# Normalising attention probabilities on GpSimd before the mix, instead of scaling the mix on VectorE

## Chip, cores and metric

One core of a Trainium2 chip runs the whole program. The metric is the device time of one execution in microseconds (us); the kernel before was run three times.

## The reference, cut to what matters

The program is a chain of attention and feed-forward layers over x of shape (2, 1024, 256), float32. The change lies in two of them, both called "local" in the kernel. Each has this attention, with 8 heads of 64 columns (D) and windows of 128 rows; a window of queries sees its own and the previous window of keys:

```python
q = l2norm(q) * qs
k = l2norm(k) * ksc
q, k = rotary_xpos(q, k)
...
sim = jnp.einsum('bhwid,bhwjd->bhwij', bq, bk)      # bq is scaled by 8
sim = jnp.where(mask, -jnp.finfo(sim.dtype).max, sim)
attn = jax.nn.softmax(sim, axis=-1)
out = jnp.einsum('bhwij,bhwjd->bhwid', attn, bv)
...
x = x + o @ wo
```

The softmax's division by the sum can be applied to the probabilities (256 columns a head and row) or, as it is linear, to the mix `out` (64 columns a head and row).

## The kernel before, in words

local_attention (L3100 on) handles 16 tiles of 128 rows (T = 16, 8 for each of the two batch entries). All engines run their own queue, written out by hand: every_step(T, (lag, body), ...) calls in each of 16 steps s the bodies in the order given, each for the tile s - lag. After the 16 steps the remaining pieces of the last tiles (LAST = 15) are listed one by one. Semaphores connect the queues; `x.at(t, name)` is the value that means "x of tile t is done".

What one tile goes through:

- TensorE: turn (L3393) transposes the input into the bank c; ScalarE's copy_h (L3322) brings it to SBUF. project_q, project_k and project_v (L3399) multiply with the weights into the banks q, k and v. project_q and project_k wait until ScalarE's copy_qk of the tile before has left these banks.
- VectorE: rope_q and rope_k (L3219, L3221, L3224) apply the rotation; norms (L3235, L3238) sums ScalarE's squares (L3353); GpSimd's power (L3169) makes the inverse norms of queries and keys; VectorE applies the keys' (L3245).
- One step later turn_qk (L3422) transposes both into the banks q and k, ScalarE's copy_qk (L3333, L3335) copies them to SBUF, and score (L3440) fills the four score banks.
- Two steps later VectorE's maxima (L3255, L3260) masks, takes row maxima and writes biases; ScalarE's exp (L3344) makes eight blocks of 128x256 probabilities, one a head, with their row sums. Semaphore steps "0" to "3" of exped mark two heads each, so that "1" means heads 0 to 3 and "3" all. turn_p (L3456) transposes the probabilities into the score banks, ScalarE's copy_p (L3359) copies them out (for the last tiles partly VectorE, L3283), mix (L3472) multiplies with the values into the bank c, and ScalarE's copy_o (L3327) copies the mix to o.
- The division: VectorE's invert (L3266) takes reciprocals of the eight sums, GpSimd's spread_inv (L3174) copies them to 64 columns a head, three steps behind TensorE's turn_inv (L3481) transposes this into the bank v in four transposes, and VectorE's scale_o (L3272) multiplies o with that bank into o_t. output (L3487) multiplies o_t with the output weights, add (L3277) adds the input, and SP shifts the result by DMAs. In layer 0 VectorE's norm_next (L3192) normalises the input of the tile after next; layer 1 has no such instruction.

TensorE's order in a step is turn, turn_qk, turn_inv, project_q, output, project_k, turn_p, project_v, mix, score. VectorE's order is maxima, scale_o, rope_q, add, norm_next, norms, invert, rope_k, and in the last two steps statistics (L3069, L3072, L3074) for the feed-forward that follows. ScalarE's order is copy_h, copy_qk, exp, square, copy_p, copy_v, copy_o. GpSimd's is spread_inv and power. A feed-forward stage follows each of the two attention stages and starts when all engines are through.

## Time and profile before

| | us |
|---|---|
| median of three runs | 2340.4 |
| lowest, highest | 2330.86, 2352.32 |
| the profiled execution, its own time | 2345.13 |
| its span in the trace | 2343.4 |

A profile shows one execution. Times in it are us from the start of the span. PE is TensorE's matmuls, PEld its weight loads, DVE VectorE, ACT ScalarE, POOL GpSimd, SP SyncE. The first local attention stage lies at about 613 to 864 us and the second at about 990 to 1245 us.

### The profile page before, as it was taken

The numbers are of one execution on the slowest core, as the hardware profiler recorded it, in microseconds if no ns is written. First come the engines' busy times: TensorE is split into PE (matmuls) and PEld (weight loads), VectorE is DVE, ScalarE is ACT, GpSimd is POOL, SyncE is SP. The second block draws the span as 40 slices with busy tenths as digits, with TensorE's granted clock in tenths as the row PEclk, the third lists the DMA queues.
The fourth block names the chain that finished last, engine by engine and source line by source line (L and its number), as shares of the span: only waits on it lengthen the run. The fifth ranks groups of instructions, "written<-read, shape, count | busy, mean of one in ns | idle before, by whom it ended". The sixth has DMA issues, their size and how long they took to land. (4 is left out here: it accounts for less than half of the span.)

```text
span 2343.4 us, 39319 instructions
## 1 busy us (share of the span) xinstructions
PE 2099.3 (90%) x12889; PEld 1560.0 (67%) x12889; DVE 1094.8 (47%) x4126; ACT 936.1 (40%) x2964; POOL 615.2 (26%) x553
## 2 busy tenths in 40 slices
PE   7888889987699989889998969969999699599998
PEld 4565548765366655556664558858887477499997
DVE  4555424438577753267773347822222355412111
ACT  3344313324377752157773225412221366333332
POOL 0455525652222210022221002222223112312222
PEclk9777779998799999999999979969999799799999
DMA  8500029988590020000000054111221801276662
GB/s 289 216 7 28 14 80 313 342 243 293 182 368 15 11 66 0 15 28 11 11 10 6 0 203 144 40 41 28 36 35 17 287 21 42 78 244 181 179 179 52
DMA packets 161423, 255.35 MB, mean 109 GB/s; under 512 B 37548, under 2 KB 123984, under 8 KB 160311
## 3 DMA queue, kind: packets, MB, share of 16 engines
q1 hardware_dynamic: 131798, 224.62, 27.8%
q0 software_dynamic: 29424, 28.21, 6.8%
q8 instruction: 107, 1.75, 0.3%
q14 instruction: 94, 0.76, 0.1%
HBM read 165.95 MB, written 101.04 MB: 114 GB/s over the span
## 5 line engine op out<-in xcount | busy, mean ns | idle before, releaser
L2736 ACT ACTIVATE m3e_ht<-m3e_h_bank,m3w_b 128x128 f32<-128x128 f32 x312 | 89.2, 368 | 189.0 <-PE m3e_h_bank L2708 187.2
L3344 ACT ACTIVATE la_probs<-la_probs,la_nb,la_invnorm 128x256 f32<-128x256 f32 x256 | 150.2, 594 | 0.0
L926 POOL DMA_INDIRECT m_xbuf<-m0w_rows,m0w_slots x128 | 127.1, 993 | 65.6 <-issue 36.3
L2719 PE MATMUL m3e_y_bank<-m3w_w,m3e_ht 128*128 x624 | 141.0, 379 | 0.0
L2890 ACT ACTIVATE m2e_ht<-m2e_h_bank,m2w_b 128x270 f32<-128x270 f32 x128 | 62.2, 487 | 179.0 <-PE m2e_h_bank L2855 179.0
L2428 POOL DMA_INDIRECT m_sum<-m0e_y,m0e_dest x64 | 98.8, 1544 | 106.6 <-DVE m0e_y L2600 75.3
L2719 PEld LDWEIGHTS m3e_y_bank<-m3w_w,m3e_ht 128*128 128x128 f32 x624 | 115.7, 190 | 14.1
L2683 POOL DMA_INDIRECT out<-m3e_y,m3e_dest x39 | 60.4, 1549 | 238.7 <-DVE m3e_y L2771 230.7
L2830 POOL DMA_INDIRECT m_sum<-m2e_y,m2e_dest x48 | 70.2, 1463 | 199.6 <-DVE m2e_y L2938 194.2
L2855 PE MATMUL m2e_h_bank<-m2e_xt,m2w_w 128*128 128x270 f32 x512 | 121.4, 395 | 0.0
L2748 DVE COPY m3e_xt<-m3e_turned_bank 128x256 f32<-128x256 f32 x39 | 16.5, 424 | 220.0 <-PE m3e_turned_bank L2696 220.0
L2865 PE MATMUL m2e_y_bank<-m2e_ht,m2w_w 128*128 128x270 f32 x512 | 119.3, 391 | 0.0
L2855 PEld LDWEIGHTS m2e_h_bank<-m2e_xt,m2w_w 128*128 128x128 f32 x512 | 96.9, 192 | 19.1
L2865 PEld LDWEIGHTS m2e_y_bank<-m2e_ht,m2w_w 128*128 128x128 f32 x512 | 96.0, 190 | 18.3
L3174 POOL COPY la_spread<-la_inv 128x512 f32<-128x512 f32 x32 | 19.5, 611 | 325.2 <-DVE la_inv L3266 325.2
L3169 POOL TENSOR_TENSOR la_invnorm<-la_clamped,all_minushalf 128x16 f32<-128x16 f32 x32 | 92.9, 2902 | 35.2 <-DVE la_clamped L3238 35.2
L3255 DVE CUSTOM_DVE_ANT_0 la_probs<-la_score_bank,lo_shut 128x256 f32<-128x256 f32 x256 | 97.9, 420 | 6.4 <-PE la_score_bank L3440 5.3
L2453 PE MATMUL m0e_gu_bank<-m0e_xt,m0w_wgu 128*128 128x128 f32 x768 | 92.5, 278 | 0.0
L2708 PE MATMUL m3e_h_bank<-m3e_xt,m3w_w 128*128 128x128 f32 x768 | 91.2, 278 | 0.2 <-DVE m3e_xt L2748 0.2
L2453 PEld LDWEIGHTS m0e_gu_bank<-m0e_xt,m0w_wgu 128*128 128x128 f32 x768 | 89.6, 194 | 0.6 <-issue 0.6
L2708 PEld LDWEIGHTS m3e_h_bank<-m3e_xt,m3w_w 128*128 128x128 f32 x768 | 89.0, 194 | 0.6 <-DVE m3e_xt L2748 0.6
L3631 PE MATMUL lf_g_bank<-lf_zt,lo_w 128*128 128x512 f32 x160 | 79.3, 620 | 7.5 <-DVEq L3549 7.5
(504 smaller groups left out, 4850.0 us busy)
## 6 DMA issues: line engine op xcount, KB each, us to landing
m3w_w<-in_m_w SPq DMA_DIRECT2D x32, 1024.0 KB, 9.4
m0w_wgu<-in_m_gu SPq DMA_DIRECT2D x32, 768.0 KB
m_xbuf<-all_zeros SPq DMA_DIRECT2D x38, 528.0 KB, 6.0
m2w_w<-in_m_w SPq DMA_DIRECT2D x16, 1024.0 KB, 12.6
m3e_w<-in_m_w SPq DMA_DIRECT2D x15, 1024.0 KB, 6.7
m0e_wd<-in_m_down SPq DMA_DIRECT2D x32, 384.0 KB
m_xbuf<-all_zeros SPq DMA_DIRECT2D x16, 576.0 KB, 7.7
m0w_xb<-m_xbuf SPq DMA_DIRECT2D x32, 288.0 KB
```

What stands on the lines that cost most here:

```text
L926: nc.gpsimd.indirect_dma_start(k.slot_buffers[m.name][0][:, :], bass.IndirectOffsetOnAxis(ahead.slots[:, t, i:i + 1], 0), ahead.rows[t % R ...
L2428: nc.gpsimd.indirect_dma_start(sums[j][:, :], bass.IndirectOffsetOnAxis(dest[q % NY][:, i:i + 1], 0), y[q % NY][:, i, :], None, bounds_che ...
L2453: last = nc.tensor.matmul(gu_ps[u][:, i * 512 + j * P:i * 512 + (j + 1) * P], wgu[q % NG][:, i * DC + c, j * P:(j + 1) * P], xt[u][:, c, i ...
L2708: last = nc.tensor.matmul(h_ps[t % 2][half][:, i * R:(i + 1) * R], w1[t % NW][:, c, f0:f0 + P], xt[t % 2][:, c, :], start=c == 0, stop=c = ...
L2719: last = nc.tensor.matmul(y_ps[t % 2][0:R, 0:D], h_t[t % 2][:, c, :], ahead.w2[:, bass.ts(e, 1), c, :].rearrange("p o f -> p (o f)"), star ...
L2736: last = nc.scalar.activation(h_t[t % 2][:, 4 * half + i, :], h_ps[t % 2][half][:, i * R:(i + 1) * R], m.act, bias=ahead.b1[:, bass.ds(e * ...
L2855: last = nc.tensor.matmul(h_ps[n % 3][:, 0:N], ahead.w1[:, h // 2, c, f * P:(f + 1) * P], xt[h % 2][:, c, :], start=c == 0, stop=c == DC - 1)
L2865: last = nc.tensor.matmul(y_ps[c][:, 0:N], ahead.w2[:, h // 2, f, c * P:(c + 1) * P], h_t[h % 2][:, f, :], start=f == 0, stop=f == HC - 1)
L3169: nc.gpsimd.tensor_tensor(inv_norm[t % 2][:, :], clamped[t % 2][:, :], k.minus_half[:, :], ALU.pow).then_inc(powered.sem, 1)
L3255: last = nc.vector.tensor_tensor_reduce(probs[u][:, hh, :], score_ps[j][:, i * 2 * P:(i + 1) * 2 * P], lo.shut[:, int(t % TB == 0), :], 1. ...
L3344: last = nc.scalar.activation(probs[u][:, hh, :], probs[u][:, hh, :], ACT.Exp, bias=nb[u][:, hh:hh + 1], scale=inv_norm[u][:, hh:hh + 1], ...
L3631: last = nc.tensor.matmul(ps[:, :], w1[:, dc, i, :], z_t[g % 2][:, dc, :], start=dc == 0, stop=dc == DC - 1)
```

## The change

The reciprocals multiply the probabilities themselves, before they are transposed. GpSimd does it in place, head by head, in eight tensor_scalar instructions of 128x256 a tile: four after the sums of heads 0 to 3 (scale_low), four after those of heads 4 to 7 (scale_high). VectorE takes the reciprocals in two halves, invert_low directly behind maxima and invert_high behind norm_next. The spread reciprocals, their transposes (turn_inv) and the scaled mix (scale_o, with the buffers spread and o) go; ScalarE copies the mix straight into o_t, and output waits for that copy. On TensorE turn_p, mix and score are split into halves, and the order of a step becomes turn, turn_qk, project_q, output, project_k, turn_low, project_v, turn_high, mix_low, score_low, mix_high, score_high. At the end of the loop the pieces keep their order, without turn_inv and scale_o, with both reciprocals of tile 14 behind the maxima of tile 15.

```diff
@@ gpsimd
-                def spread_inv(t):
-                    pool.wait_ge(inverted.sem, inverted.at(t, "inverted"))
-                    pool.wait_ge(inv_turned.sem, inv_turned.at(t - 1, "invturned"))
-                    nc.gpsimd.tensor_copy(spread[:, :, :], inv[t % 2][:, :].unsqueeze(2).broadcast_to([P, LH, LD])).then_inc(spreading.sem, 1)
+                def scale_probs(t, j):
+                    pool.wait_ge(inverted.sem, inverted.at(t, f"{j}"))
+                    for hh in range(2 * (j - 1), 2 * (j - 1) + 4):
+                        last = nc.gpsimd.tensor_scalar(probs[t % 2][:, hh, :], probs[t % 2][:, hh, :], inv[t % 2][:, hh:hh + 1], None, ALU.mult)
+                    last.then_inc(scaled.sem, 1)
...
-                every_step(T, (2, spread_inv), (0, power), (0, power_forward))
+                every_step(T, (2, scale_low), (2, scale_high), (0, power), (0, power_forward))
@@ vector
-                def invert(t):
-                    dve.wait_ge(exped.sem, exped.at(t, "3"))
-                    dve.wait_ge(spreading.sem, spreading.at(t - 2, "spreading"))
-                    nc.vector.reciprocal(inv[t % 2][:, :], total[t % 2][:, :]).then_inc(inverted.sem, 1)
-
-                def scale_o(t):
-                    dve.wait_ge(o_copied.sem, o_copied.at(t, "ocopied"))
-                    dve.wait_ge(inv_turned.sem, inv_turned.at(t, "invturned"))
-                    dve.wait_ge(made.sem, made.at(t - 1, "made"))
-                    nc.vector.tensor_tensor(o_t[:, :, :], o[:, :, :], v_ps[:, :].rearrange("p (c n) -> p c n", c=4),
-                                            ALU.mult).then_inc(o_scaled.sem, 1)
+                def invert(t, j):
+                    h0 = 2 * (j - 1)
+                    dve.wait_ge(exped.sem, exped.at(t, f"{j}"))
+                    dve.wait_ge(scaled.sem, scaled.at(t - 2, f"{j}"))
+                    nc.vector.reciprocal(inv[t % 2][:, h0:h0 + 4], total[t % 2][:, h0:h0 + 4]).then_inc(inverted.sem, 1)
...
-                every_step(T, (2, maxima), (3, scale_o), (0, rope_q), (3, add), (0, norm_next), (0, norms), (2, invert), (0, rope_k), (0, forward_stats), steps=T)
+                every_step(T, (2, maxima), (2, invert_low), (0, rope_q), (3, add), (0, norm_next), (2, invert_high), (0, norms), (0, rope_k),
+                           (0, forward_stats), steps=T)
                 maxima(LAST - 1)
-                scale_o(LAST - 2)
                 maxima(LAST)
+                invert_low(LAST - 1)
+                invert_high(LAST - 1)
                 forward.norm(dve, 0)
                 forward.norm(dve, 1)
                 add(LAST - 2)
-                invert(LAST - 1)
                 copy_p(LAST - 1, range(4))
                 for t in range(2, 4):
                     forward.stats(dve, t)
-                scale_o(LAST - 1)
-                invert(LAST)
+                invert_low(LAST)
+                invert_high(LAST)
                 copy_p(LAST, (2, 3))
                 add(LAST - 1)
                 for t in range(2, 4):
                     forward.norm(dve, t)
-                scale_o(LAST)
                 add(LAST)
@@ scalar
                 def copy_o(t):
                     act.wait_ge(mixed.sem, mixed.at(t, "mixed"))
-                    act.wait_ge(o_scaled.sem, o_scaled.at(t - 1, "oscaled"))
-                    nc.scalar.copy(o[:, :, :], c_ps[:, :].rearrange("p (c n) -> p c n", c=4)).then_inc(o_copied.sem, 1)
+                    act.wait_ge(made.sem, made.at(t - 1, "made"))
+                    nc.scalar.copy(o_t[:, :, :], c_ps[:, :].rearrange("p (c n) -> p c n", c=4)).then_inc(o_copied.sem, 1)
@@ tensor, turn_p
                         pe.wait_ge(exped.sem, exped.at(t, f"{j0 + 1}"))
+                        pe.wait_ge(scaled.sem, scaled.at(t, f"{j0 + 1}"))
@@ tensor
-                every_step(T, (0, turn), (1, turn_qk), (3, turn_inv), (0, project_q), (3, output), (0, project_k), (2, turn_p), (0, project_v), (2, mix), (1, score), steps=T)
+                every_step(T, (0, turn), (1, turn_qk), (0, project_q), (3, output), (0, project_k), (2, turn_low), (0, project_v), (2, turn_high),
+                           (2, mix_low), (1, score_low), (2, mix_high), (1, score_high), steps=T)
                 turn_qk(LAST)
-                turn_inv(LAST - 2)
                 score(LAST)
                 output(LAST - 2)
                 turn_p(LAST - 1)
...
                 mix(LAST - 1)
                 turn_p(LAST)
-                turn_inv(LAST - 1)
                 output(LAST - 1)
                 mix(LAST)
...
-                turn_inv(LAST)
                 output(LAST)
```

## Rows read from the trace of the kernel before

**Rows 1.** Page, first part: engine, busy us, share of the span, instructions.
```profile
PE 2099.3 (90%) x12889; PEld 1560.0 (67%) x12889; DVE 1094.8 (47%) x4126; ACT 936.1 (40%) x2964; POOL 615.2 (26%) x553
```

**Rows 2.** Windows: busy us (instructions) of PE, PEld, DVE, ACT, POOL; PE clock; DMA.
```profile
...
744.54:758.77 14.23, 14.17 (x134) 9.72 (x130) 11.17 (x37) 10.42 (x28) 3.47 (x2) 1.00 0.04 10
```

**Rows 3.** Timeline, a usual step of layer 0: start us, us, engine, line, out<-in.
```profile
737.01 0.59 ACT L3333 COPY la_qt<-la_q_bank 128x512 f32<-128x512 f32 x1
...
737.25 0.60 PE L3481 MATMUL la_v_bank<-all_ident,la_spread 128*128 128x128 f32 x4
...
737.75 1.96 PE L3399 MATMUL la_q_bank<-lo_wqkv,la_ht 128*128 128x512 f32 x4
...
739.02 0.69 DVE L3272 TENSOR_TENSOR la_ot<-la_o,la_v_bank 128x512 f32<-128x512 f32 x1
...
739.74 0.69 DVE L3219 TENSOR_TENSOR la_cosed<-la_q_bank,lo_cosq 128x512 f32<-128x512 f32 x1
...
740.23 0.19 ACT L3344 ACTIVATION_READ_ACCUMULATOR la_probs<-la_probs,la_nb,la_invnorm 128x1 f32 x1
...
742.13 0.41 DVE L3192 TENSOR_SCALAR lo_y<-all_x,all_mv,all_rstd 128x256 f32<-128x256 f32 x1
...
742.57 0.19 ACT L3344 ACTIVATION_READ_ACCUMULATOR la_probs<-la_probs,la_nb,la_invnorm 128x1 f32 x1
...
743.40 1.21 PE L3456 MATMUL la_score_bank<-all_ident,la_probs 64*128 64x64 f32 x32
...
745.78 2.90 POOL L3169 TENSOR_TENSOR la_invnorm<-la_clamped,all_minushalf 128x16 f32<-128x16 f32 x1
...
746.43 0.69 DVE L3224 TENSOR_TENSOR la_qk<-la_cosed,la_sined 128x512 f32<-128x512 f32 x1
```

**Rows 4.** Timeline, output in steps 3 and 15 of layer 0; idle before in brackets.
```profile
654.33 1.99 PE L3487 MATMUL la_v_bank<-lo_wo,la_ot 128*128 128x256 f32 x8 [0.65 <-DVE la_ot L3272]
...
825.93 1.99 PE L3487 MATMUL la_v_bank<-lo_wo,la_ot 128*128 128x256 f32 x8 [0.83 <-DVE la_ot L3272]
```

**Rows 5.** Groups by line of GpSimd, whole span: busy us, mean ns, idle before.
```profile
L3169 POOL TENSOR_TENSOR la_invnorm<-la_clamped,all_minushalf 128x16 f32<-128x16 f32 x32 | 92.9, 2902 | 35.2 <-DVE la_clamped L3238 35.2
...
L3174 POOL COPY la_spread<-la_inv 128x512 f32<-128x512 f32 x32 | 19.5, 611 | 325.2 <-DVE la_inv L3266 325.2
...
L3164 POOL MEMSET all_zeros<- 128x1152 f32 x1 | 1.2, 1205 | 0.0
```

**Rows 6.** Timeline, the end of layer 0's attention, tiles 14 and 15.
```profile
844.79 0.16 DVE L3260 SCALAR_TENSOR_TENSOR la_nb<-la_mx,la_invnorm 128x2 f32<-128x2 f32 x1
...
844.82 1.21 PE L3456 MATMUL la_score_bank<-all_ident,la_probs 64*128 64x64 f32 x32 [0.81 <-DVE la_mx L3255]
...
845.86 0.20 DVE L3266 RECIPROCAL la_inv<-la_total 128x8 f32<-128x8 f32 x1
...
845.98 2.43 DVE L3283 COPY la_probst<-la_score_bank 128x512 f32<-128x512 f32 x4
...
849.49 1.22 PE L3456 MATMUL la_score_bank<-all_ident,la_probs 64*128 64x64 f32 x32
...
849.95 0.15 DVE L3074 TENSOR_SCALAR lf_ve<-lf_mv 128x1 f32<-128x1 f32 x1
...
852.13 1.99 PE L3487 MATMUL la_v_bank<-lo_wo,la_ot 128*128 128x256 f32 x8 [0.84 <-DVE la_ot L3272]
...
854.05 1.97 PE L3472 MATMUL la_c_bank<-la_probst,la_v 128*64 128x128 f32 x32
...
857.13 0.58 ACT L3327 COPY la_o<-la_c_bank 128x512 f32<-128x512 f32 x1
...
858.49 1.99 PE L3487 MATMUL la_v_bank<-lo_wo,la_ot 128*128 128x256 f32 x8 [1.44 <-DVE la_ot L3272]
```

**Rows 7.** Timeline, scores of the last tile, layer 0 and layer 1.
```profile
840.03 2.06 PE L3440 MATMUL la_score_bank<-la_kt,la_qt 64*128 64x128 f32 x32 [2.00 <-DVE la_mx L3255]
...
1220.93 3.42 PE L3440 MATMUL la_score_bank<-la_kt,la_qt 64*128 64x128 f32 x32 [1.99 <-DVE la_mx L3255]
```

More of the change, by code:

```diff
@@ L3158, in _ @@
             def _(pool):
[L3159 removed]
+                for st in (powered, scaled, forward.powered):
                     pool.sem_inc(st.sem, 2 * st.n)
@@ L3432, in score @@
                     pe.wait_ge(qk_copied.sem, qk_copied.at(t, "k"))
-                    for j0 in (0, 2):
+                    for j0 in ((0, 2) if half is None else (half,)):
                         for i in range(2):
@@ L3443, in score, with score_low, score_high, turn_p @@
                                         last.then_inc(scored.sem, 1)
-                def turn_p(t):
+                def score_low(t):
+                    score(t, 0)
+                def score_high(t):
+                    score(t, 2)
+                def turn_p(t, banks=(0, 2)):
                     if t == LAST - 1:
@@ L3459, in turn_p, with turn_low, turn_high, mix @@
                                         last.then_inc(p_turned.sem, 1)
-                def mix(t):
-                    u = t % 2
+                def turn_low(t):
+                    turn_p(t, (0,))
+                def turn_high(t):
+                    turn_p(t, (2,))
+                def mix(t, chunks=range(4)):
                     pe.wait_ge(v_copied.sem, v_copied.at(t, "vcopied"))
@@ L3465, in mix @@
                     pe.wait_ge(o_copied.sem, o_copied.at(t - 1, "ocopied"))
-                    for c in range(4):
+                    for c in chunks:
                         if c % 2 == 0:
@@ L3473, in mix, with mix_low, mix_high, output @@
                                                         probs_t[:, hh, w, :], start=w == 0, stop=w == 1, skip_group_check=True)
-                    last.then_inc(mixed.sem, 1)
-                def turn_inv(t):
-                    pe.wait_ge(spreading.sem, spreading.at(t, "spreading"))
+                    if 3 in chunks:
+                        last.then_inc(mixed.sem, 1)
+                def mix_low(t):
+                    mix(t, (0, 1))
+                def mix_high(t):
+                    mix(t, (2, 3))
+                def output(t):
+                    pe.wait_ge(o_copied.sem, o_copied.at(t, "ocopied"))
                     pe.wait_ge(added.sem, added.at(t - 1, "added"))
@@ L3480, in turn_inv @@
                     for c in range(4):
-                        last = nc.tensor.transpose(v_ps[:, c * P:(c + 1) * P], spread[:, 2 * c:2 * c + 2, :].rearrange("p h e -> p (h e)"), k.ident[:, :])
-                    last.then_inc(inv_turned.sem, 1)
-                def output(t):
-                    pe.wait_ge(o_scaled.sem, o_scaled.at(t, "oscaled"))
-                    for c in range(4):
                         last = nc.tensor.matmul(v_ps[:, 0:D], o_t[:, c, :], wo[:, c, :], start=c == 0, stop=c == 3)
                     last.then_inc(made.sem, 1)
-                every_step(T, (0, turn), (1, turn_qk), (3, turn_inv), (0, project_q), (3, output), (0, project_k), (2, turn_p), (0, project_v), (2, mix), (1, score), steps=T)
+                every_step(T, (0, turn), (1, turn_qk), (0, project_q), (3, output), (0, project_k), (2, turn_low), (0, project_v), (2, turn_high),
+                           (2, mix_low), (1, score_low), (2, mix_high), (1, score_high), steps=T)
                 turn_qk(LAST)
-                turn_inv(LAST - 2)
                 score(LAST)
```

28 lines of the change are left out of this document (17 added, 11 removed).

## The prediction

> **What bounds the kernel now.** I read the page first: TensorE is busy for 90% of the span, so what counts is whether its queue ever stands still [rows 1]. The change touches only the two attention stages of the local layers, each a loop of 16 steps. The windows view over one step, cut at the start of the value projection, gives 14.23 us with TensorE busy for 14.17 of them, VectorE for 11.17, ScalarE for 10.42 and GpSimd for 3.47, at full clock [rows 2]. So in these steps TensorE has no holes, and nothing counts that doesn't shorten or interrupt its queue. The timeline of that step then says what each piece of the queue waits for [rows 3]; timelines of the first and last steps show the few holes that there are [rows 4].
>
> **Part 1, the four turns of the spread reciprocals go (turn_inv).** They take TensorE from 737.25 to the projection of the queries at 737.75 [rows 3], about 0.5 us, in steps 3 to 15 of each layer: 13 x 2 x 0.5 = 13 us if it were all won. It isn't. project_q writes the bank of the queries, so it waits for ScalarE's copy of that bank, which runs 737.01 to 737.60; its matmul starts 0.15 us after that. The turns fill a wait that stays when they go. From the copy's end with 0.06 us for the semaphore and about 0.03 for the first weight load, the projection could start about 0.06 us earlier, no more. Term: 13 x 0.06 = -0.8 us a layer. What is late next is the chain turn_qk, copy of q, project_q; the new hole of some 0.5 us has only this small value.
>
> **Part 2, VectorE's scaling of the mix goes (scale_o, 0.69 us), and output no longer waits for it.** In a usual step it runs 739.02 to 739.71 and output follows when project_q's matmuls end anyway (737.75 + 1.96 = 739.71), so nothing is won there. In step 3 TensorE stood 0.65 us for it and in step 15 0.83 us, there because VectorE had other work in front [rows 4]. These waits go: -1.5 us a layer. The pieces mix_low, score_low, mix_high, score_high hold the same matmuls as mix and score; TensorE had no wait for the copies there in a usual step, so the new order wins nothing.
>
> **Part 3, GpSimd multiplies eight 128x256 blocks a step.** The trace has no GpSimd tensor_scalar. Near rows: its copy of 128x512 takes 611 ns, 1.19 ns a column, its memset of 1152 columns 1205 ns, 1.05 a column. The other way lies its pow, 2902 ns for 16 columns [rows 5]. From below: half the copy, 0.31 us. From above: the pow's 181 ns a column would make 46 us of 256 columns (8 blocks in 16 steps of two layers: some 12 ms more). That is a power, which takes many operations an element, while a product takes one; so the value lies by far nearer to the copy, which streams one tensor as the product does. From that far end the range takes only blocks up to about 0.8 us, more than twice the copy's rate. I take 0.45 us each, half above the copy's rate, for the multiplication and the scalar of each partition. Four then take 1.8 us.
> The Trainium skill, "GPSIMD Engine Reference", section 3.1, gives about 1.8 cycles an element for a tight loop: as an estimate 384 ns for 256 elements and a little for dispatch. By it the sum below would stay the same within a microsecond; no row here shows it.
>
> Does this reach TensorE's queue? Low half: the fourth exponential's sum is read by 740.42 (740.23 + 0.19). VectorE, idle after its maxima, now waits there, takes 0.20 for the reciprocal (0.20, [rows 6]), and GpSimd starts at about 740.74 and ends at 742.54. TensorE comes to the low turns at 743.40 less 0.06 = 743.34 [rows 3]. Slack 0.8 us; it holds up to 0.64 us a block. High half: VectorE's wait delays rope_q from 739.74 to 740.68. From rope_q's start to the end of norm, with add between, are 2.80 us (739.74 to 742.13 + 0.41) [rows 3]; so the high reciprocal ends at 743.68 (the eighth exponential's sum is done at 742.57 + 0.19), GpSimd starts at 743.74 and ends at 745.54. TensorE reaches the high turns after the low turns (half of 1.21) and the value projection (1.96, as project_q): 745.9. Slack 0.3 us; it holds up to 0.52 us a block, in the second layer, where norm is absent, to 0.6. Queued behind the two new VectorE waits are rope_q, add, norm_next and the norms. rope_q's sines are still done before ScalarE's squares (742.0 against 742.66), add ends about when norm starts, 742.13 + 0.94 = 743.1, and the value projection needs it at 743.9. GpSimd's own queue behind the scaling is the pow (745.78 before, behind the spread copy); it now starts at 745.5 and isn't late. So a usual step stays at about 14.17 us.
>
> **Part 4, the end of each layer, where nothing hides GpSimd.** Times of layer 0 [rows 6]. VectorE's last bias ends at 844.95; only then come both reciprocals of tile 14 (they stand behind the maxima of tile 15). GpSimd works 845.2 to 848.8 (8 x 0.45), the high turns end at 849.5 instead of 846.03 (844.82 + 1.21). VectorE's last two of the four copies (0.61 each) end at 850.75 instead of 848.41. Its statistics keep 1.69 us (848.41 to 850.10), the reciprocals of tile 15 end at 852.65, GpSimd 852.7 to 856.3, and the turns of tile 15 end at 857.0 instead of 850.71. output(14), now behind them, starts at 856.95 instead of 852.13: +4.8 us. The mix of tile 15 moves with it from 854.05 to 858.9, ScalarE's copy from 857.13 to 861.95, ending 862.54, and the last output starts at 862.6 instead of 858.49, as scale_o is no more between: +4.1 us a layer. With 0.31 us a block it would be 16 x 0.14 = 2.2 us less, +1.9.
> TensorE now stands about 2 us before each of the two turns. After such a hole the scores of the last tile took 3.42 us in layer 1, and 2.06 in layer 0 [rows 7]: a lower clock costs up to 1.4 us a time. I take one such loss, +1.4; between 0 and 4 x 1.4.
>
> **Sum.** A layer: -0.8 - 1.5 + 4.1 = +1.8, two layers +3.6, clock +1.4: +5 us. The profiled execution took 2345.1 us (span 2343.4), so 2350.1; the median of the three runs is 4.7 us below it, so 2345 on that scale. A measurement of this kernel can tell about 1% (23 us; the runs shown lie 21 us apart), so I forecast no change.
>
> **Rivals.**
> A, GpSimd is slow (slower). If a block takes 0.8 us, low scaling ends at 743.94 and the low turns wait 0.66 us; the high scaling then runs to 747.14 while TensorE is there at 746.6: another 0.6. Some 1.3 us in each of the 14 steps from step 2 of both layers is 36 us, the ends take 16 x 0.35 x 2 = 11.2 more: 2345 + 47 = 2392 us. It decides from about 0.66 us a block (there 9 us in the steps and 7 at the ends beyond the forecast's +5). For it: pow shows that GpSimd's arithmetic can be far from its copy. Against it: copy and memset both run near 1.1 ns a column. 0.20.
> B, GpSimd and VectorE hinder each other. rope_q's last addition (0.69 us, two tensors of SBUF) would fall in the low scaling, which would end at 743.23, still before 743.34; the addition itself may wait for one block, so the high scaling ends 0.45 later at 745.99, TensorE waits 0.2 us, in 14 steps of two layers 5.6 us: 2351 us; with blocks of 0.6 us it would be some 0.9 us a step, 2370. Against it: the pow (745.78 to 748.68) overlaps such an addition in every step, at 746.43 for instance, which takes the same 0.69 us as other 512-column operations [rows 3]. The Trainium skill, "SBUF — State Buffer", says that a VectorE instruction with two SBUF inputs and a GpSimd instruction that reads SBUF exclude one another for their whole length; the trace has only the pow beside it and shows no such price. 0.15.
> C, the freed 0.5 us is won in full: 13 x 2 x 0.44 = 11 us more, 2334 us. This needs ScalarE's copy to end before TensorE is through with the turns, and rows 3 speak against it. 0.05.
> D, the loop isn't as tight as drawn and 0.7 us a step goes somewhere: faster by over 1%. Nothing shows it. 0.04.
>
> **How the numbers follow.** Forecast 0.56, A 0.20, B 0.15, C 0.05, D 0.04. Forecast, C and nearly all of B lie within 1%; A and a small part of B are slower by more, as are blocks between 0.5 and 0.66 us with a bad clock: 0.23. Faster 0.04, same 0.73. The range goes from 2326 (C and the scatter of the runs) to 2390 (most of A).
>
> **What would show it.** The step's pitch stays between 14.1 and 14.3 us with 13.6 us of TensorE busy in it; TensorE waits for ScalarE's query copy before project_q, about 0.5 us; waits for GpSimd at the low and high turns are zero in the steps and 1.5 to 3 us four times at the layers' ends; the scaling blocks measure 0.4 to 0.5 us. A pitch near 13.7 would make part 1 wrong, waits of turn_low or turn_high in every step part 3, an unmoved end of the layers part 4.

## The result, and the profile after

| | us |
|---|---|
| before, median (lowest, highest) of 3 runs | 2340.4 (2330.86, 2352.32) |
| after, median (lowest, highest) of 3 runs | 2464.86 (2462.63, 2465.87) |
| ratio after / before, 95% interval | 1.0517 [1.0478, 1.0555] |
| the profiled execution after, its own time and span | 2465.87, 2464.1 |

The change makes the kernel 5.2% slower; the profiled execution takes 120.7 us more than that of before (2345.13). I had forecast 2345 us, no change, and the time lies beyond my range (2326 to 2390). It went the way of rival A, and further than A's price.

The page of after, its first part and then the two groups of the change (GpSimd's scaling, TensorE's turns of the probabilities):

```profile
span 2464.1 us, 39398 instructions
...
PE 2113.9 (86%) x12761; PEld 1565.5 (64%) x12761; DVE 1075.7 (44%) x4126; ACT 933.4 (38%) x2964; POOL 844.6 (34%) x777
...
L3173 POOL TENSOR_SCALAR la_probs<-la_probs,la_inv 128x256 f32<-128x256 f32 x256 | 247.3, 985 | 209.1 <-DVE la_inv L3273 209.1
...
L3469 PE MATMUL la_score_bank<-all_ident,la_probs 64*128 64x64 f32 x1024 | 48.8, 238 | 108.6 <-POOL la_probs L3173 108.6
```

TensorE's busy time rose by only 14.6 us against [rows 1], while the span rose by 120.7: most of the loss is TensorE standing. The second group puts 108.6 us of it down to waits for GpSimd's scaling. The first group has the reason: a block takes 985 ns in the mean, where I had reckoned 450.

The windows view of one step, cut as [rows 2] at the start of the value projection:

```profile
754.24:771.76 17.52, 14.21 (x130) 9.57 (x127) 10.45 (x37) 10.36 (x27) 10.77 (x10) 1.00 0.03 9
```

TensorE still does 14.21 us of work at full clock, but the step takes 17.52 instead of 14.23. GpSimd went from 3.47 us to 10.77. The waits of this stretch, in total, times, longest:

```profile
DVE la_qk L3251 <- POOL la_invnorm L3168: 4.7, 1, 4.7
...
PE la_score_bank L3469 <- POOL la_probs L3173: 3.0, 2, 1.5
...
PE la_q_bank L3405 <- ACT la_qt L3339: 0.3, 1, 0.3
```

14.21 + 3.0 + 0.3 = 17.5: the step is accounted for. Its timeline, a usual step of layer 0 as in [rows 3]:

```profile
746.00 0.59 ACT L3339 COPY la_qt<-la_q_bank 128x512 f32<-128x512 f32 x1
...
746.74 1.96 PE L3405 MATMUL la_q_bank<-lo_wqkv,la_ht 128*128 128x512 f32 x4 [0.33 <-ACT la_qt L3339]
...
749.44 0.18 DVE L3273 RECIPROCAL la_inv<-la_total 128x4 f32<-128x4 f32 x1 [2.15 <-ACT la_probs L3350]
...
749.72 7.88 POOL L3173 TENSOR_SCALAR la_probs<-la_probs,la_inv 128x256 f32<-128x256 f32 x8 [6.75 <-DVE la_inv L3273]
...
750.91 0.73 DVE L3230 TENSOR_TENSOR la_qk<-la_cosed,la_sined 128x512 f32<-128x512 f32 x1
...
752.22 0.16 DVE L3273 RECIPROCAL la_inv<-la_total 128x4 f32<-128x4 f32 x1
...
753.59 0.71 PE L3469 MATMUL la_score_bank<-all_ident,la_probs 64*128 64x64 f32 x16 [1.46 <-POOL la_probs L3173]
...
755.22 0.69 DVE L3230 TENSOR_TENSOR la_qk<-la_cosed,la_sined 128x512 f32<-128x512 f32 x1
...
757.57 2.92 POOL L3168 TENSOR_TENSOR la_invnorm<-la_clamped,all_minushalf 128x16 f32<-128x16 f32 x1
757.74 0.71 PE L3469 MATMUL la_score_bank<-all_ident,la_probs 64*128 64x64 f32 x16 [1.52 <-POOL la_probs L3173]
```

The high reciprocal is ready at 752.38, when the low scaling still runs; so the eight blocks follow one another without a gap, 7.88 us, and TensorE stands 1.46 us at the low turns and 1.52 at the high ones. VectorE's scaling of the keys, which waits 4.7 us for the pow behind these blocks, ends at 761.28, before TensorE turns the keys in the next step, and costs nothing.

Six of the eight blocks take 0.92 us. The third takes 1.02, beside VectorE's norm_next (a tensor_scalar, 751.90 to 752.30); without norm_next, in layer 1, a step is 0.1 us shorter. The seventh stands out; the same timeline of GpSimd alone, at 755.23:

```profile
755.23 1.47 POOL L3173 TENSOR_SCALAR la_probs<-la_probs,la_inv 128x256 f32<-128x256 f32 x1
```

It begins 0.01 us behind rope_k's last addition (755.22, two operands of SBUF) and takes 0.55 us more than the others.

The end of layer 0, the part that answers to [rows 6] (with the scores of the last tile, [rows 7], first):

```profile
888.11 3.65 PE L3446 MATMUL la_score_bank<-la_kt,la_qt 64*128 64x128 f32 x32 [1.95 <-DVE la_mx L3261]
...
893.87 0.28 DVE L3273 RECIPROCAL la_inv<-la_total 128x4 f32<-128x4 f32 x2
...
894.15 7.35 POOL L3173 TENSOR_SCALAR la_probs<-la_probs,la_inv 128x256 f32<-128x256 f32 x8 [8.94 <-DVE la_inv L3273]
...
898.05 0.95 PE L3469 MATMUL la_score_bank<-all_ident,la_probs 64*128 64x64 f32 x16 [4.37 <-POOL la_probs L3173]
...
901.65 1.12 PE L3469 MATMUL la_score_bank<-all_ident,la_probs 64*128 64x64 f32 x16 [2.65 <-POOL la_probs L3173]
...
905.97 7.21 POOL L3173 TENSOR_SCALAR la_probs<-la_probs,la_inv 128x256 f32<-128x256 f32 x8 [4.46 <-DVE la_inv L3273]
...
909.73 1.11 PE L3469 MATMUL la_score_bank<-all_ident,la_probs 64*128 64x64 f32 x16 [3.35 <-POOL la_probs L3173]
...
913.32 1.12 PE L3469 MATMUL la_score_bank<-all_ident,la_probs 64*128 64x64 f32 x16 [2.48 <-POOL la_probs L3173]
...
914.37 3.78 PE L3506 MATMUL la_v_bank<-lo_wo,la_ot 128*128 128x256 f32 x8
```

The four waits at the turns are those that I had drawn, only longer, and the clock falls beside them. Windows over two of these rows (before the last two numbers stands the granted clock):

```profile
888.00:891.70 3.70, 3.59 (x33) 3.50 (x33) 1.50 (x11) 3.70 (x14) 0.00 (x0) 0.54 0.00 0
...
914.40:918.20 3.80, 3.80 (x12) 2.61 (x12) 1.30 (x3) 0.00 (x0) 0.00 (x0) 0.50 0.00 0
```

The scores of the last tile and the output run near or at 1.2 GHz, half the full clock: 3.65 us where before had 2.06, 3.78 where before had 1.99. For the scores the record doesn't show that this comes from the change: TensorE stood as long ahead of them before (2.00 us), and in layer 1 they took 3.42 us before and 2.91 after.

From TensorE's first turn to the last addition, layer 0 took 247.9 us before (613.09 to 860.94) and takes 308.1 now (616.48 to 924.57): +60.2, half of the whole loss. Fourteen steps at 3.29 us each (17.52 - 14.23) are 46 of it; 14 are left for the end and the first steps. Layer 1, where a step takes 17.42 us, gives +57.4 in the same way.

### The profile page after: what moved, and what is told of

Read it like the earlier page. It is cut to its first block and busy times, and to the rows that moved or that the text cites. A ratio compares the mean times of both kernels' runs of the same rounds, so it can differ in the third digit from the quotient of the medians.

```text
span 2464.1 us, 39398 instructions
## 1 busy us (share of the span) xinstructions
PE 2113.9 (86%) x12761; PEld 1565.5 (64%) x12761; DVE 1075.7 (44%) x4126; ACT 933.4 (38%) x2964; POOL 844.6 (34%) x777
## 5 line engine op out<-in xcount | busy, mean ns | idle before, releaser
L3173 POOL TENSOR_SCALAR la_probs<-la_probs,la_inv 128x256 f32<-128x256 f32 x256 | 247.3, 985 | 209.1 <-DVE la_inv L3273 209.1
L3469 PE MATMUL la_score_bank<-all_ident,la_probs 64*128 64x64 f32 x1024 | 48.8, 238 | 108.6 <-POOL la_probs L3173 108.6
L3469 PEld LDWEIGHTS la_score_bank<-all_ident,la_probs 64*128 64x128 f32 x1024 | 41.4, 148 | 156.5 <-issue 156.5
L2719 PEld LDWEIGHTS m3e_y_bank<-m3w_w,m3e_ht 128*128 128x128 f32 x624 | 115.7, 190 | 14.1
L3365 ACT COPY la_probst<-la_score_bank 128x512 f32<-128x512 f32 x116 | 62.3, 589 | 133.3 <-PE la_score_bank L3469 133.3
```

The costliest lines, as they stand in the source:

```text
L2719: last = nc.tensor.matmul(y_ps[t % 2][0:R, 0:D], h_t[t % 2][:, c, :], ahead.w2[:, bass.ts(e, 1), c, :].rearrange("p o f -> p (o f)"), star ...
L3173: last = nc.gpsimd.tensor_scalar(probs[t % 2][:, hh, :], probs[t % 2][:, hh, :], inv[t % 2][:, hh:hh + 1], None, ALU.mult)
L3469: last = nc.tensor.transpose(score_ps[j0 + half][:, c0:c0 + QH], probs[t % 2][q0:q0 + QH, 2 * j0 + i, w * P:(w + 1) * P], k.ident[q0:q0 + ...
```

## The experiments

The theory after this reading: GpSimd's block is too long (0.92 us alone), and rope_k's addition holds one of eight for another 0.55. Rivals: the new order of the pieces costs by itself; or the block's length is a price of the instruction as such, and not of its columns. "Pitch" is the time from one step to the next in the middle of layer 0. The runs were compared with the kernel before on the same chip.

### e1_one_column: GpSimd scales one column of each head

```diff
-                        last = nc.gpsimd.tensor_scalar(probs[t % 2][:, hh, :], probs[t % 2][:, hh, :], inv[t % 2][:, hh:hh + 1], None, ALU.mult)
+                        last = nc.gpsimd.tensor_scalar(probs[t % 2][:, hh, 0:1], probs[t % 2][:, hh, 0:1], inv[t % 2][:, hh:hh + 1], None, ALU.mult)
```

The other 255 columns stay without their reciprocal. Every instruction, wait and place in the order stays.

> GpSimd scales one column of each head instead of 256, so most of the normalisation is left out; queues, waits and order are those of the changed kernel. Theory L (the loss is GpSimd's block of 0.98 us, which stands before both turns of every step and 16 times in a row at each layer's end): the step's pitch falls from 17.52 us to 14.1-14.2 us, both waits for GpSimd in a step are gone, the 0.3-0.5 us wait of project_q for ScalarE's copy of the queries stays, and the time is about 2332-2340 us, within 0.5% of the kernel before. Rival O (the loss lies in the new order, in VectorE's early wait for the exponentials or in the halves): the pitch stays above 15 us and the time above 2370 us. Rival F (the removed turns are a gain of 0.5 us a step that the scaling hides): pitch 13.7 us, about 2325 us.

Measured: 2344.41 us, ratio 0.9993 [0.9965, 1.002], pitch 14.40. A block:

```profile
L3173 POOL TENSOR_SCALAR la_probs<-la_probs,la_inv x256: 272/282/420, 639.1 to 1235.2; 128x1 f32<-128x1 f32 x128
```

The waits for GpSimd in the steps are gone, and with them the whole loss. The new order by itself makes no difference to the time that these runs can tell. The pitch is 0.17 us above that of before, where I had expected 14.1 to 14.2 us (see e5 and e9).

### e2_half_width: 128 of 256 columns

Edit: as e1, with `0:P`. Half of each head's columns stays unscaled.

> GpSimd scales 128 of the 256 columns of each head (half of the normalisation is left out). If a block costs by its columns it takes 0.45-0.55 us, the length on which the forecast was built. Theory L: pitch 14.2 to 14.4 us, waits for GpSimd in a step at most 0.2 us, time 2340-2355 us, so the schedule of the prediction was right and only the block's length wrong. Rival O (order): pitch above 15 us. If the block has a large fixed cost (0.7 us or more for half the columns) the pitch is 15 us or more, with the waits at the turns to show it.

Measured: 2387.06 us, 1.018 [1.0139, 1.0221], pitch 15.22. My expectation missed (2340 to 2355 us, pitch 14.2 to 14.4): a block takes a little longer than I had set, and something else comes with it.

```profile
L3173 POOL TENSOR_SCALAR la_probs<-la_probs,la_inv x256: 592/601/1111, 637.1 to 1268.3; 128x128 f32<-128x128 f32 x128
```

With 272, 592 and 912 ns at the least for 1, 128 and 256 columns, both halves give 2.5 ns a column (320 / 127 and 320 / 128) on 0.27 us that don't depend on them. So it is a straight line, more than twice as steep as the copy of [rows 5] (1.19 ns a column).

The longest block, 1111 ns, shows what else there is. A step of this run, the block from GpSimd's timeline:

```profile
791.67 1.11 POOL L3173 TENSOR_SCALAR la_probs<-la_probs,la_inv 128x128 f32<-128x128 f32 x1
...
791.69 0.70 DVE L3230 TENSOR_TENSOR la_qk<-la_cosed,la_sined 128x512 f32<-128x512 f32 x1
...
793.65 0.71 PE L3469 MATMUL la_score_bank<-all_ident,la_probs 64*128 64x64 f32 x16 [0.74 <-POOL la_probs L3173]
```

Here the held block is one of the low half, beside rope_q's addition, and TensorE stands 0.74 us at the low turns and not at all at the high ones. The block is 0.51 us too long, and the one behind it, beside norm_next, takes 0.75 us, 0.15 too long. So 0.66 of the 0.74 us is VectorE's doing: with undisturbed blocks of 0.60 us TensorE would have stood under 0.1 us. That is rival B in its own place, and near the 0.9 us a step that it set for blocks of 0.6.

### e4_end_only: full width only for the last two tiles

```diff
+                        cols = 2 * P if t >= LAST - 1 else 1
-                        last = nc.gpsimd.tensor_scalar(probs[t % 2][:, hh, :], ...
+                        last = nc.gpsimd.tensor_scalar(probs[t % 2][:, hh, 0:cols], ...
```

Tiles 0 to 13 stay unscaled but for a column.

> GpSimd scales all 256 columns only for the last two tiles (14 and 15) of each layer and one column for the others (the normalisation of the others is left out). Against the run with one column everywhere this gives the price of the layers' ends alone. Theory L: 16 blocks of 0.92 us stand on the path of each end, 14-15 us a layer less what hides there, so 24-30 us over the one-column run, about 2362 us. Rival (the ends hide the blocks behind the last maxima and exponentials): under 8 us over the one-column run.

Measured: 2366.19 us, 1.0089 [1.0055, 1.0122], pitch 14.40 as e1. The two ends cost 2366.19 - 2344.41 = 22 us, a little less than the 24 to 30 that I had expected; the steps cost the rest.

### e3_short_add: both rope additions cut to 64 columns

```diff
-                    nc.vector.tensor_tensor(qk[:, i, :].rearrange("p (h e) -> p h e", h=LH), cosed[:, i, :, :], sined[:, i, :, :],
-                                            ALU.add).then_inc(roped.sem, 1)
+                    nc.vector.tensor_tensor(qk[:, i, 0:LD], cosed[:, i, 0, :], sined[:, i, 0, :], ALU.add).then_inc(roped.sem, 1)
```

Seven of eight heads' queries and keys stay at zero (one memset ahead of the loop); the scaling is that of the change.

> The two additions of the rotation on VectorE (two SBUF inputs, 512 columns, 0.69 us) are cut to 64 columns; the rest of the queries and keys is left out (zero). GpSimd's blocks stay 256 columns. Theory C (the block that starts right behind such an addition is held for it: one block of the eight takes 1.47 us instead of 0.92): no block above 1.05 us, the eight take 7.3-7.5 us instead of 7.88, pitch about 17.0 us, time 14-18 us below the changed kernel, about 2448 us. Rival (the long block has another cause, or the length is the engine's own scatter): long blocks stay, pitch 17.4-17.5 us, time unchanged.

Measured: 2440.72 us, 1.0417 [1.0374, 1.0459], pitch 17.06. That is 0.46 us a step less than the change, some 13 us in 28 steps. The median is 24 us lower, more than the 14 to 18 that I had expected, but not all of it is the edit's: from the first turn of layer 0 to the last addition of layer 1 the profiled run took 735.6 us (605.73 to 1341.32), against 745.8 after the change (616.48 to 1362.27), 10 us less, and another 11 were gone ahead of that first turn. The block's span of lengths shows where the 0.46 us come from; the first row is the change, the second this run:

```profile
L3173 POOL TENSOR_SCALAR la_probs<-la_probs,la_inv x256: 912/922/1476, 644.6 to 1350.6; 128x256 f32<-128x256 f32 x128
```

```profile
L3173 POOL TENSOR_SCALAR la_probs<-la_probs,la_inv x256: 913/922/1053, 634.2 to 1328.7; 128x256 f32<-128x256 f32 x128
```

The longest goes from 1476 to 1053 ns (blocks of this length lie beside norm_next, one of 1.03 us at 704.64), and the median stays. TensorE's two waits tell which addition it is:

```profile
706.71 0.72 PE L3469 MATMUL la_score_bank<-all_ident,la_probs 64*128 64x64 f32 x16 [1.46 <-POOL la_probs L3173]
...
710.39 0.72 PE L3469 MATMUL la_score_bank<-all_ident,la_probs 64*128 64x64 f32 x16 [1.05 <-POOL la_probs L3173]
```

At the low turns, beside rope_q's addition, nothing changed (1.46); at the high turns, beside rope_k's, 1.52 became 1.05. So with blocks of 0.92 us it is rope_k's addition that costs. The shorter addition also makes VectorE's own queue shorter; that doesn't reach the eight blocks, which run without a gap either way. In both runs in which a block is held (e2, the change) the addition and the block start within 0.02 us of one another; rope_q's addition in the change starts 0.28 us into a block and no block is held.

### e6_filler: four transposes back where turn_inv was

One column as in e1, and TensorE turns the identity four times into the bank of the values between turn_qk and project_q.

```diff
+                def filler(t):
+                    pe.wait_ge(added.sem, added.at(t - 1, "added"))
+                    pe.wait_ge(v_copied.sem, v_copied.at(min(t + 2, T - 1), "vcopied"))
+                    for c in range(4):
+                        nc.tensor.transpose(v_ps[:, c * P:(c + 1) * P], k.ident[:, :], k.ident[:, :])
-                every_step(T, (0, turn), (1, turn_qk), (0, project_q), (3, output), ...
+                every_step(T, (0, turn), (1, turn_qk), (3, filler), (0, project_q), (3, output), ...
```

> One column scaled (normalisation left out), and four transposes of the identity into the value bank stand between turn_qk and project_q, where the turns of the reciprocals had been. Hidden wait: these four, 0.5 us by themselves, cost at most 0.15 us a step (pitch 14.4-14.55 us), project_q's wait for the copy is gone. Rival F (the turns' time counts in full): pitch 14.9 us, 13 us more.

Measured: 2346.22 us, 1.0112 [0.9962, 1.0261] (the interval is wide and says little), pitch 14.40, as e1 to the hundredth. The turns and what stands behind them:

```profile
781.22 0.60 PE L3505 MATMUL la_v_bank<-all_ident 128*128 128x128 f32 x4
781.72 1.96 PE L3405 MATMUL la_q_bank<-lo_wqkv,la_ht 128*128 128x512 f32 x4
```

The wait for the query copy is gone and the pitch has not moved: the four turns fill exactly the hole that they leave.

### e5_output_first: that hole filled with output

One column as in e1, and output stands ahead of project_q.

```diff
-                every_step(T, (0, turn), (1, turn_qk), (0, project_q), (3, output), (0, project_k), ...
+                every_step(T, (0, turn), (1, turn_qk), (3, output), (0, project_q), (0, project_k), ...
```

> One column scaled (normalisation left out), and TensorE's output stands before project_q. In the one-column run the pitch is 14.40 us, and project_q starts 0.94 us behind the last turn of the keys, with a wait of 0.33 us for ScalarE's copy of the queries. If that wait is a true hole which the removed turns of the reciprocals had filled, output fills it: pitch 14.0-14.1 us, no such wait, about 8 us less than the one-column run. Rival (the wait is a mark of the profile and the turns were a true gain): pitch unchanged at 14.4 us.

Measured: 2335.43 us, 1.0003 [0.9952, 1.0055], pitch 14.11 by this window:

```profile
778.20:792.31 14.11, 13.87 (x127) 9.48 (x127) 10.34 (x38) 10.19 (x28) 5.03 (x9) 1.00 0.04 10
```

That is 0.29 us a step less than e1, so output did have slack to be moved; the value projection then waits 0.24 us for the addition instead. Eight microseconds in all are below what the scatter of these runs lets one tell (2320 to 2346).

### e9_whole: mix and score whole again

One column as in e1, with mix and score undivided behind turn_high.

> One column scaled (normalisation left out), and TensorE's mix and score are whole again (turn_p stays in halves around the value projection). In the one-column run the four halves take 4.23 us from the first mix to the next turn, the whole ones of the kernel before 3.88, with the same matmuls. If each change between groups of matmuls costs TensorE about 0.1 us, the pitch falls from 14.40 to 14.05-14.25 us (the second half of mix may now wait up to 0.2 us for the last copy of the probabilities). Rival (the extra 0.17 us over the kernel before has another source, VectorE's early wait or the late copies): pitch 14.4 us or more.

Measured: 2343.26 us, 1.0001 [0.9972, 1.0031], pitch 14.41: the expectation missed. Making mix and score whole wins nothing. TensorE in a step of e9:

```profile
781.42 0.71 PE L3469 MATMUL la_score_bank<-all_ident,la_probs 64*128 64x64 f32 x16
782.07 2.33 PE L3490 MATMUL la_c_bank<-la_probst,la_v 128*64 128x128 f32 x32
```

The whole mix takes 2.33 us here, against 1.97 in before ([rows 6]), as its last weight loads wait 0.4 us for ScalarE's last copy of the turned probabilities; mix and score together take 4.24 us from start to start (782.07 to 786.31). That copy is later because turn_high stands directly ahead of mix instead of a value projection. The halves hide this wait and pay for it otherwise: in e1 the four half pieces take 4.23 us from start to start (787.60 to 791.83), the two whole ones in before 3.88. In e9 the wait is the whole excess of 0.36 us over before; what the 0.35 us of e1 consist of, these runs don't separate.

### e7_vector and e8_split: the scaling on VectorE, and shared

Both compute everything. e7 puts the eight blocks on VectorE, directly behind each reciprocal; e8 gives two heads of each half to VectorE and two to GpSimd.

```diff
+                    for hh in range(h0, h0 + 4):
+                        last = nc.vector.tensor_scalar(probs[t % 2][:, hh, :], probs[t % 2][:, hh, :], inv[t % 2][:, hh:hh + 1], None, ALU.mult)
+                    last.then_inc(scaled.sem, 1)
```

> VectorE scales all eight blocks itself, behind each half's reciprocals; GpSimd keeps only the power. Full computation. VectorE's 128x256 tensor_scalar took 0.41 us with two scalars (0.34 apart); at 0.33 us a block a half costs 1.3 us in place of GpSimd's 3.7-4.1, but it stands in VectorE's own queue before rope_q and the norms: the two waits for the scaling at the turns are gone, add and the rotation come 1.3-2.6 us later, and the pitch is 14.5-15.0 us, 2355-2380 us. If a block takes 0.2 us or less, pitch 14.4 us, within 0.5% of the kernel before. Rival (the block on GpSimd isn't what costs, but the wait of TensorE for any scaling at all): pitch above 16 us.

> Of each half VectorE scales two heads and GpSimd two at the same time. Full computation. By length alone GpSimd's part is 1.84 us a half, 8 us in all at the ends: pitch 14.6-15.0 us, about 2365-2380 us. If the two engines exclude one another while VectorE's one-input instruction runs, GpSimd's first block of each half is held by up to 0.7 us and blocks of 1.3 us or more show beside it: pitch 15.3 us or more.

Measured: e7 2367.31 us, 1.0187 [1.0053, 1.0321], pitch 14.93, within its expectation. e8 2368.8 us, 1.0203 [1.0064, 1.0342], pitch 15.20, above the 14.6 to 15.0 that I expected without mutual hindrance; the blocks of 1.3 us or more that I expected with it don't show either. The block on VectorE in e7, then in e8:

```profile
L3276 DVE TENSOR_SCALAR la_probs<-la_probs,la_inv x256: 345/349/355, 645.6 to 1261.0; 128x256 f32<-128x256 f32 x128
```

```profile
L3277 DVE TENSOR_SCALAR la_probs<-la_probs,la_inv x128: 352/461/572, 625.8 to 1245.9; 128x256 f32<-128x256 f32 x128
...
L3174 POOL TENSOR_SCALAR la_probs<-la_probs,la_inv x128: 914/958/1089, 625.9 to 1247.6; 128x256 f32<-128x256 f32 x128
```

VectorE needs 0.35 us for what takes GpSimd 0.92. When both scale at once, each is longer, VectorE by 0.11 us in the median, GpSimd by 0.04. That is small beside e8's loss: TensorE stands 0.49 us at its high turns and 0.18 us for the addition. e7 loses its time elsewhere: the addition is late behind the scaling, and the value projection waits 0.5 us for it.

### e12_tt_by_head and e10_tensor_tensor: another instruction for the same product

Both compute everything, on GpSimd, with a tensor_tensor whose second operand is the reciprocal broadcast over the columns: e12 in eight blocks of 256 columns, e10 in two of 1024.

```diff
+                        last = nc.gpsimd.tensor_tensor(probs[t % 2][:, hh, :], probs[t % 2][:, hh, :], inv[t % 2][:, hh:hh + 1].broadcast_to([P, 2 * P]), ALU.mult)
```

```diff
+                    h0 = 2 * (j - 1)
+                    nc.gpsimd.tensor_tensor(probs[t % 2][:, h0:h0 + 4, :], probs[t % 2][:, h0:h0 + 4, :],
+                                            inv[t % 2][:, h0:h0 + 4].unsqueeze(2).broadcast_to([P, 4, 2 * P]), ALU.mult).then_inc(scaled.sem, 1)
```

> GpSimd scales each half in one tensor_tensor of 128x1024 with the reciprocals broadcast, in place of four tensor_scalar. Full computation. The blocks of 1, 128 and 256 columns took 0.28, 0.60 and 0.92 us, so 0.27 us fixed and 2.5 ns a column. If the rate per column is the same and the fixed part falls due once, a half takes 2.8-2.9 us instead of 3.7: pitch 15.6-16.0 us, about 2410-2425 us. If two inputs from SBUF cost GpSimd more a column than one, 4 us or more a half: pitch 17.5 us or more, no better than the changed kernel.

> Eight tensor_tensor of 128x256 a tile, each with one head's reciprocal broadcast, in place of eight tensor_scalar. Full computation. The 128x1024 tensor_tensor took 1.90 us, 1.85 ns a column at most, while tensor_scalar has 2.5 ns a column and 0.27 us fixed. Theory K (the kind of instruction decides, and its fixed cost is small): a block takes 0.5-0.6 us, pitch 14.8-15.2 us, about 2370-2385 us. Rival M (merging four heads decides): a block takes 0.75 us or more, pitch 16 us or more.

Measured: e10 2367.64 us, 1.0094 [1.0063, 1.0125], pitch 14.78; e12 2385.78 us, 1.0155 [1.0115, 1.0194], pitch 15.09, as theory K had it. Block lengths of e12 and of e10:

```profile
L3173 POOL TENSOR_TENSOR la_probs<-la_probs,la_inv x256: 606/613/1062, 651.8 to 1280.4; 128x256 f32<-128x256 f32 x128
```

```profile
L3173 POOL TENSOR_TENSOR la_probs<-la_probs,la_inv x64: 1893/1894/1944, 642.3 to 1253.0; 128x1024 f32<-128x1024 f32 x64
```

The same eight products take 0.61 us a head instead of 0.92 when only the kind of instruction is changed, and 0.47 a head in one instruction of four heads. e10 did better than I expected (2410 to 2425): 0.47 us is the length of my prediction, so e10 is the test of its schedule. It comes out 0.9% slower than before. In layer 0 TensorE stands 0.31 us a step at the high turns; in layer 1, which has no norm_next, it doesn't stand there, and the pitch is 14.46. The timeline of layer 0 shows who is held now:

```profile
789.78 1.89 POOL L3173 TENSOR_TENSOR la_probs<-la_probs,la_inv 128x1024 f32<-128x1024 f32 x1 [6.62 <-DVE la_inv L3273]
...
790.99 1.23 DVE L3230 TENSOR_TENSOR la_qk<-la_cosed,la_sined 128x512 f32<-128x512 f32 x1
...
793.04 1.89 POOL L3173 TENSOR_TENSOR la_probs<-la_probs,la_inv 128x1024 f32<-128x1024 f32 x1 [1.37 <-DVE la_inv L3273]
...
794.16 0.80 DVE L3244 TENSOR_SCALAR la_clamped<-la_ss 128x16 f32<-128x16 f32 x1
...
795.08 0.71 PE L3469 MATMUL la_score_bank<-all_ident,la_probs 64*128 64x64 f32 x16 [0.31 <-POOL la_probs L3173]
```

rope_q's addition begins while GpSimd's instruction runs and takes 1.23 us, 0.54 more than alone; it ends 0.55 us after GpSimd's instruction does (789.78 + 1.89 = 791.67, 790.99 + 1.23 = 792.22). It stands ahead of the high reciprocal, which is late by it. In e12 the same addition takes 1.09 us, and TensorE stands 0.49 us at the low turns.

### e11_tt_output_first: e10 with output ahead of project_q

Edit: e10's and e5's together; it computes everything.

> One tensor_tensor a half, and TensorE's output before project_q. Full computation. The run with one column gained 0.29 us a step by that order, since output fills the wait for ScalarE's copy. Here, if the wait for the high half (0.31 us a step) stays and only the hole is filled: pitch 14.5 us, 2355-2362 us. If the loop is bound by VectorE and GpSimd (the chain from the exponentials over rope_q, which is held for the scaling, to the high half), TensorE only waits longer there: pitch 14.7-14.8 us, 2365 us.

Measured: 2367.76 us, 1.0105 [1.0073, 1.0136], pitch 14.78, as e10; the second of the two expectations. What output wins ahead, TensorE waits again at the high turns (0.4 us instead of 0.3). The pitch is the same though TensorE's hole is filled, so the loop of layer 0 no longer turns at TensorE's pace; that it turns at that of exponentials, VectorE held by GpSimd, reciprocals, scaling and turns fits the rows and is argued, not tested by a run of its own.

## Why the prediction was wrong

**The step that failed** is Part 3's term "I take 0.45 us each, half above the copy's rate". A block took 0.985 us in the mean, 0.92 undisturbed. I had put the product near the copy, as both stream one tensor. By e2 its slope is 2.5 ns a column where the copy has at most 1.19, and 0.27 us come on top that the copy's mean couldn't show, since I divided it by its columns and had but one size of it. My rows did not exclude this: I had the pow as the upper end (46 us) and cut the range at 0.8 us by judgment, with no row behind the cut. The Trainium skill ("GPSIMD Engine Reference", section 3.1), whose 1.8 cycles an element I had quoted, calls them the best case, that of a tight loop. At the 1.2 GHz that the same section gives, 2.5 ns are 3.0 cycles, so this instruction was far from that case. By the estimate of 384 ns alone my sum would have been 2 x 16 x 0.066 = 2.1 us lower, not the same within a microsecond. The Trainium skill's 2.6 cycles there for a tensor_tensor, an addition, are above what e10's product shows (1.85 ns a column, 2.2 cycles).

**The schedule around it held in the main.** I had GpSimd start 2.99 us behind project_q (740.74 against 737.75); it starts 2.98 behind (749.72 against 746.74). With 0.985 us a block the rival A's own arithmetic gives 2.1 us more work ahead of the low turns, less the slack of 0.8: a wait of 1.3 (measured 1.46), and 1.4 more at the high turns (measured 1.52). That is 2.7 us in 28 steps, 76 us, and 17 at the ends; with the forecast's +5 some 98 of the measured 121. So the mechanism of A was right, its decision point of 0.66 us was passed, and its price of 0.8 us was too low. At the low turns the agreement is partly luck: the four blocks there end 3.72 us behind their start (753.44), which gives 1.1 and not 1.3. The rest is that TensorE is ready for them 5.39 us behind the start of project_q (752.13), where I had 5.59, and that the turns start 0.15 us behind the last block (753.59).

**Where the 121 us are.** Fourteen steps at 3.29 us and fourteen at 3.19 (layer 1) are 91. Of the 3.29, 2.98 are the two waits, of which e3 removes 0.46 by taking the addition away, and 0.17 is the order's (e1's pitch). The last 0.14 belongs to the waits too: the view counts a wait from the modelled end of the piece before, and without a wait the next piece starts 0.07 us ahead of that end (e1: 784.40 against 782.59 + 1.88 = 784.47), twice a step. The ends: e4 prices their blocks at 22 us over e1's, against my +4.1 a layer and +1.4 of clock. 16 blocks at 0.47 us too much are 7.5 a layer, and in layer 0 scores, output and three turns lose some 1.6, 1.8 and 1.2 us at 1.2 GHz, where I had allowed one loss of 1.4. Steps and ends are 113. From the first turn of layer 0 to the last addition of layer 1 the loss is 116.5 us (613.09 to 1242.35 before, 616.48 to 1362.27 after), so some 3 in the two layers stay open; the other 4 of the 121 lie outside, 3.4 of them ahead of that first turn, where the two kernels are the same.

**Rival B** was true as well. I had looked at rope_q's addition beside the low scaling, and with blocks of 0.60 us it costs just there, 0.5 us a step (e2). With 0.92 us a block it changes nothing (e3); what costs then is rope_k's, which I had standing well behind the scaling, as 0.45 us a block would have had it: the high scaling would have ended ahead of it. Slower blocks made these two meet. "The trace shows no such price" was drawn from the pow, which overlaps an addition without harm in [rows 3]; it was not a sample of an instruction that streams a tensor. The Trainium skill ("SBUF — State Buffer", "Who interferes with whom") has the rule that I weighed and left at 0.15, that whoever issues first keeps the shared ports for its whole instruction and the other blocks. Two rows nearly agree: the block at 755.23 is held 0.55 of the addition's 0.69 us, and e10's addition, which by the rule would end 0.69 us behind GpSimd's instruction, ended 0.55 behind. The addition at 750.91, which began within a running block of 0.92 us and took 0.73, does not. In e2 the block is the one held although its row begins 0.02 us ahead of the addition's; starts so near don't tell who issued first.

**Part 1** held: 0.33 us of wait stay and the turns' removal was worth 0.00 us a step (e6), my 0.06 being at the edge of what can be read. Rival C is out by the same run. **Part 2** was wrong in "nothing is won there": the time from project_q to output falls from 2.01 to 1.79 us from start to start, and that from output to project_k from 1.83 to 1.73. In [rows 3] scale_o ended at 739.71 as well, the moment at which project_q's matmuls did; I took the second for the cause, and the gain fits the first, though no run takes scale_o out alone. But "the new order wins nothing" was too kind by more: turns in halves cost 0.15 us and the pieces from mix to the next turn 0.35, and instead of a pitch of 14.1 to 14.3 us 14.40 came out. TensorE was busy for 14.07 us of it, where I had set 13.6 as a sign. **Part 4** had the right four waits, and its length only was off. The late pow, set at nothing, does cost nothing in the steps.

**Would the forecast have been right with 0.45 us?** Nearly, and not quite. e10 has 0.47 us a head and a ratio of 1.0094 [1.0063, 1.0125], some 22 us: about at the bound of 1%, where I had said +5 us, and clearly not 0. Some 11 of the 22 are in the steps (14 x 0.55 in layer 0, 14 x 0.23 in layer 1), where I had hoped for a small gain: 0.17 a step is the order's and nearly all the rest the wait at the high turns of layer 0. The other half is mostly the ends, for which I had 9.6. e10 differs from the change in its instruction too, and blocks of 0.45 us each were never run; e2's, with 0.60, make it likely that rope_q's addition would have held one of them as well. e7, e8, e10 and e12 show no placing of this work that was free, on GpSimd or VectorE, and none beat the kernel before. A turn of the probabilities one step later, with a third buffer for them, might hide the scaling on GpSimd; it was not tried.

## What to carry to other kernels

Before moving work to an engine, measure the very instruction at two sizes: a copy's rate says neither the fixed part nor the slope of an operation with a scalar of each partition, and here they doubled the estimate. Multiply that length by the count in a row, and compare with the slack between the operand's arrival and its reader: four blocks of 0.92 us against 2.6 us was decided at once, whatever share of GpSimd's span was free. Ask of both engines which instructions will start together, too: at 0.60 us a block most of the loss in the steps was one block held beside an addition. And put the factor where the tensor is small: 64 columns of mix a head cost VectorE 0.69 us a tile (with a copy on GpSimd and four turns that both lay in holes), the same division on 256 columns of probabilities 7.9 us of GpSimd.

## What the runs showed of the hardware

- GpSimd's tensor_scalar with a scalar of each partition: 0.27 us fixed and 2.5 ns a column of 128 partitions (e1, e2, the change). Its tensor_tensor with a broadcast operand is faster, 0.61 against 0.92 us for 256 columns, and 1.85 ns a column in one piece of 1024. I would have expected the opposite, with two tensors to read.
- A GpSimd block that starts 0.01 us behind VectorE's addition of two SBUF tensors takes 1.47 us instead of 0.92; one of 128 columns that starts 0.02 us ahead of such an addition takes 1.11 instead of 0.60 (e2). Beside norm_next's tensor_scalar a block takes 1.02 instead of 0.92. The other way round, VectorE's addition takes 1.23 us instead of 0.69 behind a 1.9 us tensor_tensor, and even its 128x16 tensor_scalar, with one input, takes 803 ns in the median of e10 where e1 and before have 174. GpSimd's pow beside such an addition shows nothing of it.
- At the end of layer 0 TensorE stood 2.5 to 4.4 us ahead of each half of the turns, and most pieces behind ran at 1.2 GHz (granted clock 0.50): 1.12 us for sixteen turns that take 0.71 at the full clock, 3.78 for an output that takes 1.99.
